# A graph-network kernel on one Trainium2 core: a later part's order of work, its loads and its last operations rearranged

## The chip, the cores and the metric

The kernel runs on one core of a Trainium2 chip. A core has five engines with queues of their own, which wait for each other by semaphores: PE (TensorE, matrix products into eight PSUM banks), DVE (VectorE), ACT (ScalarE), POOL (GpSimd, which here issues the gathers) and SP (SyncE, which issues most loads). The metric is the device time of one execution, in microseconds (us); lower is better.

## The reference, cut to what matters

x is 512 x 1024 in f32; 8192 edges (src, dst), sorted by dst, connect 512 nodes. `gnn` is the reference's first layer, cut to its formulas:

```python
h = relu(layernorm(x))
feat = concat([h[src], h[dst]], axis=1)
e_f = relu(feat @ W_kind + b_kind)          # kinds: first 256 edges hh, next 1280 oo, the rest ho
logit = e_f @ W_a + b_a
alpha = exp(logit - max[dst]); alpha = alpha / segment_sum(alpha, dst)[dst]
z_f = segment_sum(alpha * h[src], dst)
new = relu(concat([h, z_f]) @ W_node + b_node)   # W_hn for rows 0..127, W_on for the rest
x = x + new
h = relu(layernorm(x))
hW = h @ W.T + b
x = x + segment_sum(deg^-1/2[row] * deg^-1/2[col] * hW[col], row)   # with self loops
```

## The kernel before

**Edges.** The edges are handled in 64 tiles of 128: tiles 0 to 51 are kind ho, 52 to 61 oo, 62 and 63 hh. For the first two kinds the products of h with the halves of the weights are made once per node and stored as two tables in HBM (`tab_a`, `tab_b`). POOL gathers, for tile q, 128 rows of `tab_a` into a slot of `gath` (line 402) and then adds 128 rows of `tab_b` to it by a second, accumulating gather (`gather_add`, line 416), which first waits for the landing of the first. Odd tiles under 52 (`PLAIN`) gather both into two slots instead (lines 402 and 409). `gath` has `GB` = 9 slots, used in turn; a gather first waits until the tile that used its slot nine uses ago has been read by DVE (`slot_free`). The order on POOL is: first gather of q, then `gather_add` of q - 2 (`LAG`).

**One list of steps.** Behind the tables, PE, ACT and DVE walk through the same list of positions (c, k), with c a chunk of products and k = 0..7. Each engine executes in order, so what stands at a position holds up all that stands behind it on that engine. In chunks 12 and 13 PE also multiplies the node weights (line 845, fed by `round_w` on ACT, line 581, and `low_w` on DVE, line 1180). Chunks 14 and 15 hold no such products. At each position DVE does, in this order: `low_w`, `copy_kind`, `edge`, `split_logits`, `logit_onehots`.

- `edge(q)` (lines 1200 to 1205) waits for the gather of tile q, takes the relu, multiplies by W_a and sums to 128 logits. `EDGE_AT` (lines 506 to 511) says at which position. A plain tile takes one more operation.
- `split_logits` (line 1226 on, `SPLIT_AT`) cuts the logits into three bf16 parts `lgs`.
- `logit_onehots(q)` (lines 1242 to 1248) makes one-hot matrices of a tile's src and dst. For the tiles in `SCALED` (57, 59, 61) DVE also multiplies by the three parts (line 1245, three operations); for all others ACT does, in `logit_parts` (line 641, three operations), behind the one-hot's semaphore.
- `sums` on PE (line 795) adds a tile's logits, as products of one-hots, to a 512 x 512 matrix of logits for its kind. The order is `SUM_AT`: ..., 44 to 49, 62, 63, 50, 51, ..., 60, 61; it and the place of the one-hots are not touched.
- `copy_kind` on DVE (line 1270) brings a finished kind's four banks to SBUF with their row maxima; kind 1 (oo) is complete with the sum of tile 61.

**Behind the edges.** `head_rows` (line 1006) is a product of the first 128 rows of h in f32 with W_hn, 16 products by k (n = 0, 1). Its weights lie in the eight slots `raw`: those of n = 0 are loaded by SP once edge 55 is done, those of n = 1 and then the next weights (`load_behind_head`, line 323), each when the product that used the slot is done. Four of the 16 stand at position (15, 1), ahead of the sums of tiles 60 and 61. Then DVE and ACT make the softmax (lines 732, 736, 1400 to 1407), PE transposes the attention (line 1023) and multiplies it by h (line 1035, below called the z products), which it needs as two parts in rows, `hrow_h` and `hrow_l`. These lie over slots 1 to 8 of `gath` and are brought back from HBM by POOL: eight loads of 512 KB that wait for all edges and for the fourth head product (lines 455 to 459). Then follow the other node products (line 845), the residual and the second norm, the spreading of rows along edges (line 1066), the product with W (lines 845 and 1088), and the output (`outputs`, lines 1517 to 1532): from each bank two DVE operations with a wait between them, then a store by SP (line 345).

Of the kernel before, what the change touches and what calls it, by code (L numbers as in the profile page):

```python
# [5 lines left out]
P = 128  # L6
FB = 512
ALU = mybir.AluOpType
# [17 lines left out]
def gnn_kernel(nc, x, src, dst, W_hh, b_hh, W_oo, b_oo, W_ho, b_ho, W_a, b_a,  # L26
# [3 lines left out]
    NM = N // P  # L30
    KT = D // P
# [7 lines left out]
    with ExitStack() as ctx:  # L39
# [22 lines left out]
        hrow = sb("hrow", [P, NM, D], F32)  # L62
# [5 lines left out]
        GB = 9  # L68
# [282 lines left out]
        def _(pool):  # L351
# [103 lines left out]
            pool.wait_ge(s_edge, TG + GB)  # L455
            pool.wait_ge(s_hn, KT // 2)
            for m in range(NM):
                pool.dma_start(hrow_h[:, m, :], h_hi[m * P:(m + 1) * P, :]).then_inc(s_hld[m], 16)
                pool.dma_start(hrow_l[:, m, :], h_lo[m * P:(m + 1) * P, :]).then_inc(s_hld[m], 16)
# [46 lines left out]
        EDGE_AT |= {divmod(12 * KT + (3 * i) // 2, KT): (41 + i,) for i in range(10)}  # L506
        EDGE_AT |= {(14, k): (51 + k,) for k in range(KT)}
        EDGE_AT |= {(15, 0): (59,), (15, 1): (60, 61)}
# [25 lines left out]
        SCALED = (57, 59, 61)  # L534
# [241 lines left out]
        def _(pe):  # L776
# [234 lines left out]
            for c in (14, 15):  # L1011
                for k in range(KT):
                    sums(c, k)
                    if (c, k) == (15, 1):
                        head_rows(0, range(4))
            head_rows(0, range(4, KT))
# [75 lines left out]
        def _(dve):  # L1092
# [5 lines left out]
            def step(ins):  # L1098

                chain[0] += 1  # L1100
                ins.then_inc(s_v, 1)
                dve.wait_ge(s_v, chain[0])
# [413 lines left out]

            def outputs(n):
                c = slice(n * FB, (n + 1) * FB)
                if n == 0:
                    chunk_done(dve, q)  # L1520
                for m in range(NM):
                    if n:
                        dve.wait_ge(s_lastbank, m + 1)
                    step(nc.vector.scalar_tensor_tensor(out=topsum[:, m, c], in0=bias2[:, 0, c], scalar=wrow[:, m:m + 1],
                                                        in1=ps[:, n * NM + m, :], op0=ALU.mult, op1=ALU.add))
                    nc.vector.scalar_tensor_tensor(out=topsum[:, m, c], in0=topsum[:, m, c], scalar=dinv[:, m:m + 1],
                                                   in1=hrow[:, m, c], op0=ALU.mult, op1=ALU.add).then_inc(s_out, 1)

            outputs(0)
# [23 lines left out]
```

## Time and profile before

| | |
|---|---|
| median of 3 runs | 578.4 us (574.28 to 585.87) |
| profiled execution | 578.26 us |
| its span, first to last instruction | 576.5 us |
| its mean granted TensorE clock | 0.973 of full |
| VectorE busy | 418.3 us (73%) |
| GpSimd busy | 192.8 us (33%) |

The span is measured from the first to the last instruction; 1.8 us of the execution lie outside it. All places below are in us from the span's start. The profile's sections give busy time by engine, the granted clock by slice, the DMA queues (q0: POOL's; q1: SP's), the chain of work that ended last, and groups of instructions by line.

### The profile page before, as it was taken

To read this page: it belongs to the slowest core of one execution; us is meant where nothing else is said; L and a number is where in the kernel's file an instruction comes from. 1 tells how busy PE (TensorE), PEld (TensorE's weight loads), DVE (VectorE), ACT (ScalarE), POOL (GpSimd) and SP (SyncE) were. 2 spreads that over 40 slices of the span, in tenths; PEclk is the share of its full clock that TensorE was granted. 3 is DMA by queue.
4 is the path that set the end of the run, shared out by engine and by line. 5 is a ranking of instruction groups with operands and counts; after the bars stand their busy time and mean duration, and the time that the engine had idled before them with its cause. 6 is when DMAs were issued, how large, how long until landed. Compare 5 with 4: busy or idle time off the path is not lost.

```text
span 576.5 us, 7188 instructions
## 1 busy us (share of the span) xinstructions
PE 519.5 (90%) x2120; PEld 359.7 (62%) x2125; DVE 418.3 (73%) x883; ACT 273.1 (47%) x432; POOL 192.8 (33%) x177
## 2 busy tenths in 40 slices
PE   0799989999998799979999799996778999999997
PEld 0688857777764467644444368672226878878885
DVE  6766347874669789789888697589897389888262
ACT  1733431211223898945644662899366274144200
POOL 3290030007466475536655644584031000000000
PEclk9999999999999899998999977998899999999999
DMA  8899286449999999999999999999596575304021
GB/s 302 315 329 399 108 279 226 131 146 247 397 343 342 344 357 279 348 318 338 370 344 350 366 337 323 216 237 281 157 354 259 213 249 192 107 2 133 14 91 55
DMA packets 55838, 146.95 MB, mean 255 GB/s; under 512 B 6770, under 2 KB 6898, under 8 KB 55410
## 3 DMA queue, kind: packets, MB, share of 16 engines
q0 software_dynamic: 22352, 81.28, 45.7%
q1 hardware_dynamic: 27936, 54.54, 26.7%
q10 hardware_dynamic: 5506, 10.56, 5.0%
q8 instruction: 27, 0.44, 0.3%
q14 instruction: 17, 0.14, 0.1%
HBM read 127.47 MB, written 18.87 MB: 254 GB/s over the span
## 4 chain that ended last, share of the span: by engine, by line
PE 59%; DVE 16%; DMA 10%; ACT 7%; issue 5%; POOL 2%; ACTq 0%; DVEq 0%
PE ps L845 37%; PE ps L795 7%; DMA gath<-tab_a,tabl_i 6%; PE ps L1035 4%; PE ps L1088 4%; PE ps L1066 3%; DVE ring_l L1180 2%; ACT late_onehots L641 2%; ACT onehot L641 2%; DMA gath<-tab_b,tabl_i 2%; DVE gath L1205 1%; DVE logit_d L1400 1%; DMA raw<-in_L_gnn_W_on_dram 1%; DVE stats L1147 1%; POOL gath L409 1%
## 5 line engine op out<-in xcount | busy, mean ns | idle before, releaser
L845 PE MATMUL ps<-ring_h,actT_h 128*128 128x512 f32 x376 | 160.8, 428 | 7.5 <-DVE actT_l L1175 3.1
L845 PE MATMUL ps<-ring_l,actT_h 128*128 128x512 f32 x376 | 148.7, 395 | 0.0
L845 PE MATMUL ps<-ring_h,actT_l 128*128 128x512 f32 x376 | 148.7, 395 | 0.0
L641 ACT ACTIVATE onehot<-onehot,lgs 128x512 bf16<-128x512 bf16 x156 | 99.9, 711 | 45.9 <-DVE onehot L1248 38.7
L581 ACT CAST ring_h<-raw 128x512 fp32r<-128x512 f32 x128 | 76.2, 623 | 91.1 <-PE ps L845 63.6
L1180 DVE TENSOR_TENSOR ring_l<-raw,ring_h 128x512 fp32r<-128x512 f32 x128 | 85.4, 687 | 44.4 <-ACT ring_h L581 32.6
L402 POOL DMA_INDIRECT gath<-tab_a,tabl_i x62 | 66.9, 1079 | 100.1 <-DVE gath L1205 48.9
L416 POOL DMA_INDIRECT gath<-tab_b,tabl_i x36 | 64.9, 1801 | 87.5 <-DMA tab_b<-stage 43.6
L1205 DVE SCALAR_TENSOR_TENSOR gath<-gath,wa_b 128x1024 f32<-128x1024 f32 x62 | 75.8, 1225 | 21.0 <-DMA gath<-tab_b,tabl_i 20.1
L845 PEld LDWEIGHTS ps<-ring_h,actT_h 128*128 128x128 f32 x376 | 72.1, 192 | 30.3 <-DVE actT_l L1175 3.3
L845 PEld LDWEIGHTS ps<-ring_h,actT_l 128*128 128x128 f32 x376 | 71.8, 191 | 16.0
L845 PEld LDWEIGHTS ps<-ring_l,actT_h 128*128 128x128 f32 x376 | 72.1, 192 | 14.3
L795 PE MATMUL ps<-onehot 128*128 128x512 bf16 x230 | 64.5, 391 | 17.1 <-ACT onehot L641 13.7
L795 PEld LDWEIGHTS ps<-onehot 128*128 128x128 bf16 x233 | 19.1, 99 | 56.1 <-issue 45.1
L1200 DVE TENSOR_TENSOR gath<-gath 128x1024 f32<-128x1024 f32 x26 | 31.7, 1220 | 3.5 <-DMA gath<-tab_b,tabl_i 3.3
L409 POOL DMA_INDIRECT gath<-tab_b,tabl_i x26 | 30.4, 1170 | 7.9 <-issue 7.3
L943 PE MATMUL ps<-raw,featT_src 128*128 128x512 f32 x64 | 30.1, 610 | 0.0
L943 PE MATMUL ps<-raw,featT_dst 128*128 128x512 f32 x64 | 29.1, 592 | 0.0
L1128 DVE TENSOR_SCALAR onehot<-iota_f,node_f 128x512 bf16<-128x512 f16 x44 | 16.1, 367 | 14.4 <-PE ps L795 12.6
L599 ACT COPY stage<-ps 128x512 f32<-128x512 f32 x16 | 9.4, 585 | 24.7 <-PE ps L845 19.0
L943 PEld LDWEIGHTS ps<-raw,featT_src 128*128 128x128 f32 x64 | 12.7, 199 | 12.8 <-issue 11.2
L1006 PE MATMUL ps<-raw,hT 128*128 128x512 f32 x32 | 17.1, 669 | 3.5 <-DMA raw<-in_L_gnn_W_hn_dram 3.1
(206 smaller groups left out, 684.5 us busy)
## 6 DMA issues: line engine op xcount, KB each, us to landing
raw<-in_L_gnn_W_ho_dram SPq DMA_DIRECT2D x32, 256.0 KB
raw<-in_L_gnn_W_oo_dram SPq DMA_DIRECT2D x32, 256.0 KB
raw<-in_L_gnn_W_hh_dram SPq DMA_DIRECT2D x32, 256.0 KB
raw<-in_L_gnn_W_on_dram SPq DMA_DIRECT2D x32, 256.0 KB
raw<-in_L_gnn_W_hn_dram SPq DMA_DIRECT2D x32, 256.0 KB
tab_a<-stage ACTq DMA_DIRECT2D x16, 256.0 KB
tab_b<-stage ACTq DMA_DIRECT2D x16, 256.0 KB
raw<-in_L_gnn_W_dram SPq DMA_DIRECT2D x16, 256.0 KB
```

The source lines that it names most:

```text
L402: pool.indirect_dma_start(out=gath[:, c % GB, :], out_offset=None, in_=tab_a[0:kinds * N, :], in_offset=bass.IndirectOffsetOnAxis(ap=tabl_ ...
L409: pool.indirect_dma_start(out=gath[:, c % GB, :], out_offset=None, in_=tab_b[0:kinds * N, :], in_offset=bass.IndirectOffsetOnAxis(ap=tabl_ ...
L416: pool.indirect_dma_start(out=gath[:, c % GB, :], out_offset=None, in_=tab_b[0:kinds * N, :], in_offset=bass.IndirectOffsetOnAxis(ap=tabl_ ...
L581: nc.scalar.copy(ring_h[:, k, :], raw[:, k % RAW, :]).then_inc(s_high, 1)
L641: ins = nc.scalar.mul(place[:, 1 + i, :], place[:, 1, :], lgs[:, i, q:q + 1])
L795: mm = nc.tensor.matmul(ps[:, bass.ds(((lo + j) & 3) + first if first else (lo + j) & 3, 1), :].rearrange("p a n -> p (a n)"), rows[:, 1 + ...
L845: mm = nc.tensor.matmul(ps[:, first + m, :], w, v, start=(k == 0 and i == 0), stop=(k == KT - 1 and i == 2))
L943: mm = nc.tensor.matmul(ps[:, b, :], featT[half][:, k, t * P:(t + 1) * P], raw[:, k, :], start=(half == 0 and k == 0), stop=(half == 1 and ...
L1035: mm = nc.tensor.matmul(ps[:, f, :], w, v, start=(k == 0 and i == 0), stop=(k == NM - 1 and i == 2))
L1180: nc.vector.tensor_tensor(ring_l[:, k, :], raw[:, k % RAW, :], f32(ring_h[:, k, :]), ALU.subtract).then_inc(s_low, 1)
L1200: nc.vector.tensor_tensor(gath[:, c % GB, :], gath[:, c % GB, :], gath[:, d % GB, :], ALU.add).then_inc(s_sum, 1)
L1205: nc.vector.scalar_tensor_tensor(out=gath[:, c % GB, :], in0=gath[:, c % GB, :], scalar=0.0, in1=wa_b[:, :], op0=ALU.max, op1=ALU.mult, ac ...
```

## The change

1. **Edges.** `EDGE_AT` puts tiles 43 to 61 one to three positions further forward. Tiles 47 and 48 go from chunk 13 into chunk 12, 51 to 53 from chunk 14 to (13, 4), (13, 5) and (13, 7), 59 to 61 from chunk 15 to (14, 5), (14, 6) and (14, 7). One-hots, splits and sums stay.
2. **Scaling.** `SCALED` holds only tile 61; tiles 57 and 59 are scaled by ACT.
3. **Head.** Two instead of four head products stand ahead of the sums of tiles 60 and 61.
4. **Loads of h.** Each of the eight waits only for the edge that frees the slot it overwrites, in the order of the last nine uses: `hrow_h` blocks 2 and 3 behind edges 53 and 54, `hrow_l` 0 to 3 behind 56 to 59, `hrow_h` 0 and 1 behind 60 and 61. They stand behind the last `gather_add` on POOL, as before.
5. **Output.** The part that needs no PSUM (bias times a row factor plus the residual) is made by eight operations ahead of the outputs; from each bank one operation is left.

```diff
-            pool.wait_ge(s_edge, TG + GB)
-            pool.wait_ge(s_hn, KT // 2)
-            for m in range(NM):
-                pool.dma_start(hrow_h[:, m, :], h_hi[m * P:(m + 1) * P, :]).then_inc(s_hld[m], 16)
-                pool.dma_start(hrow_l[:, m, :], h_lo[m * P:(m + 1) * P, :]).then_inc(s_hld[m], 16)
+            for c in range(len(USES) - GB, len(USES)):
+                slot, q = c % GB, USES[c][0]
+                if slot == 0:
+                    continue
+                part, held = (hrow_l, h_lo) if slot <= NM else (hrow_h, h_hi)
+                m = (slot - 1) % NM
+                pool.wait_ge(s_edge, GB + q + 1)
+                pool.dma_start(part[:, m, :], held[m * P:(m + 1) * P, :]).then_inc(s_hld[m], 16)
...
-        EDGE_AT |= {divmod(12 * KT + (3 * i) // 2, KT): (41 + i,) for i in range(10)}
-        EDGE_AT |= {(14, k): (51 + k,) for k in range(KT)}
-        EDGE_AT |= {(15, 0): (59,), (15, 1): (60, 61)}
+        EDGE_AT |= {(12, k): (41 + k,) for k in range(KT)}
+        EDGE_AT |= {(13, k): (49 + i,) for i, k in enumerate((1, 2, 4, 5, 7))}
+        EDGE_AT |= {(14, k): (54 + k,) for k in range(KT)}
...
-        SCALED = (57, 59, 61)
+        SCALED = (61,)
...
                     if (c, k) == (15, 1):
-                        head_rows(0, range(4))
-            head_rows(0, range(4, KT))
+                        head_rows(0, range(2))
+            head_rows(0, range(2, KT))
...
+            step(nc.vector.tensor_tensor(wrow[:, :], wrow[:, :], dinv[:, :], ALU.mult))
+            def residuals(n):
+                c = slice(n * FB, (n + 1) * FB)
+                for m in range(NM):
+                    ins = nc.vector.scalar_tensor_tensor(out=topsum[:, m, c], in0=bias2[:, 0, c], scalar=wrow[:, m:m + 1],
+                                                         in1=hrow[:, m, c], op0=ALU.mult, op1=ALU.add)
+                step(ins)
             def outputs(n):
...
-                    step(nc.vector.scalar_tensor_tensor(out=topsum[:, m, c], in0=bias2[:, 0, c], scalar=wrow[:, m:m + 1],
-                                                        in1=ps[:, n * NM + m, :], op0=ALU.mult, op1=ALU.add))
-                    nc.vector.scalar_tensor_tensor(out=topsum[:, m, c], in0=topsum[:, m, c], scalar=dinv[:, m:m + 1],
-                                                   in1=hrow[:, m, c], op0=ALU.mult, op1=ALU.add).then_inc(s_out, 1)
+                    nc.vector.scalar_tensor_tensor(out=topsum[:, m, c], in0=ps[:, n * NM + m, :], scalar=dinv[:, m:m + 1],
+                                                   in1=topsum[:, m, c], op0=ALU.mult, op1=ALU.add).then_inc(s_out, 1)
+            residuals(0)
+            residuals(1)
             outputs(0)
             outputs(1)
```

## Rows read from the trace of the kernel before

**Rows 1.** The page's first part: busy us, share of the span, instructions of each engine.
```profile
PE 519.5 (90%) x2120; PEld 359.7 (62%) x2125; DVE 418.3 (73%) x883; ACT 273.1 (47%) x432; POOL 192.8 (33%) x177
```
**Rows 2.** The chain that ended last: start, us, what; from 410 on.
```profile
410.23 2.74 PE ps L795 x6
412.97 3.77 PE ps L1006 x8
416.74 1.31 PE ps L795 x6
418.08 0.69 DVE logit_d L1270
...
438.78 22.06 PE ps L1035 x96
```
**Rows 3.** Timeline of ACT: start, us, line, operation, operands, count, [idle before <-releaser].
```profile
375.81 7.46 ACT L641 ACTIVATE onehot<-onehot,lgs 128x512 bf16<-128x512 bf16 x12 [0.76 <-DVE onehot L1248]
...
397.47 7.45 ACT L641 ACTIVATE onehot<-onehot,lgs 128x512 bf16<-128x512 bf16 x12
...
412.54 1.95 ACT L641 ACTIVATE late_onehots<-late_onehots,lgs 128x512 bf16<-128x512 bf16 x3 [3.02 <-DVE late_onehots L1248]
```
**Rows 4.** Timeline of DVE, from 354 to 411, the rows that the steps use.
```profile
354.10 0.16 DVE L1376 COPY rs_in<-ps 128x4 f32<-128x4 f32 x1 [3.49 <-PE ps L973]
...
364.80 0.69 DVE L1180 TENSOR_TENSOR ring_l<-raw,ring_h 128x512 fp32r<-128x512 f32 x1 [4.66 <-ACT ring_h L581]
...
397.13 0.17 DVE L1226 TENSOR_SCALAR lgs<-lg 128x2 uint32<-128x2 uint32 x1
...
397.93 0.35 DVE L1242 TENSOR_SCALAR onehot<-iota_f,node_f 128x512 bf16<-128x512 f16 x1
...
398.99 1.22 DVE L1205 SCALAR_TENSOR_TENSOR gath<-gath,wa_b 128x1024 f32<-128x1024 f32 x1
...
402.13 1.05 DVE L1245 TENSOR_SCALAR late_onehots<-iota_f,node_f,lgs 128x512 bf16<-128x512 f16 x3
...
409.82 1.23 DVE L1205 SCALAR_TENSOR_TENSOR gath<-gath,wa_b 128x1024 f32<-128x1024 f32 x1
```
**Rows 5.** Timeline of POOL: an awaited slot, adds of tiles 58, 59, 61, first h load.
```profile
370.51 0.97 POOL L402 DMA_INDIRECT gath<-tab_a,tabl_i  x1 [4.59 <-DVE gath L1205]
...
386.61 1.54 POOL L416 DMA_INDIRECT gath<-tab_b,tabl_i  x1 [0.30 <-issue]
...
390.22 1.98 POOL L416 DMA_INDIRECT gath<-tab_b,tabl_i  x1 [0.68 <-DMA gath<-tab_a,tabl_i]
...
398.90 2.71 POOL L416 DMA_INDIRECT gath<-tab_b,tabl_i  x1 [3.40 <-DMA gath<-tab_a,tabl_i]
...
417.28 0.62 POOL L458 DMA_DIRECT2D hrow_h<-h_hi  x1 [15.67 <-PE ps L1006]
```
**Rows 6.** The instructions of tile gath, 330 to 415: from issue to landing.
```profile
DMA to landing us min/median/max: 9.3/10.4/11.5
```
**Rows 7.** Busy by stretch; its last three columns: granted clock, DMA share, GB/s.
```profile
358.00:376.00 18.00, 17.24 (x74) 12.69 (x73) 11.48 (x30) 12.42 (x21) 11.14 (x9) 0.97 0.90 202
```
**Rows 8.** SP's DMA queue, 380 to 400: packets, MB, share of 16 engines.
```profile
q1 hardware_dynamic: 323, 0.60, 8.6%
```
**Rows 9.** Busy by stretch again, here for PE and its granted clock (last but two).
```profile
352.00:359.00 7.00, 7.00 (x23) 5.94 (x23) 4.87 (x10) 1.09 (x2) 2.42 (x2) 0.51 1.04 324
...
406.50:410.20 3.70, 0.71 (x3) 0.10 (x1) 3.61 (x11) 1.95 (x3) 0.00 (x0) 0.99 0.61 162
410.30:413.60 3.30, 3.30 (x8) 1.36 (x9) 3.13 (x12) 1.06 (x2) 0.00 (x0) 0.51 0.00 0
```
**Rows 10.** Timeline of PE: the last two head products.
```profile
430.90 3.63 PE L1006 MATMUL ps<-raw,hT 128*128 128x512 f32 x4 [0.81 <-DMA raw<-in_L_gnn_W_hn_dram]
```
**Rows 11.** Timeline of DVE: the two operations of the last output bank.
```profile
572.43 0.75 DVE L1524 SCALAR_TENSOR_TENSOR topsum<-bias,wrow,ps 128x512 f32<-128x512 f32 x1 [3.90 <-PE ps L1088]
573.21 0.75 DVE L1526 SCALAR_TENSOR_TENSOR topsum<-topsum,dinv,hrow 128x512 f32<-128x512 f32 x1
```

## The prediction

> **What bounds it now.** I read the page's busy times first: PE 519.5 us, 90% of the span [rows 1]. The change touches no weight product, so it can only gain where the chain of waits leaves PE, and that chain was read next. From 376 to 405 it lies on ACT: the scaling of one-hots starts at 375.81 and the last unbroken group ends at 397.47 + 7.45 = 404.92, so the 15 tiles 44 to 49, 62, 63, 50 to 56 take 29.1 us with the bank copies between them, 7.45 / 4 = 1.86 a tile [rows 3]. After that DVE is late: ACT waits 3.02 for the one-hot of tile 60 and ends it at 412.54 + 1.95 = 414.49 [rows 3], for DVE is still reading edges at 409.82 + 1.23 [rows 4]. PE is later still: between sums 58/59 and 60/61 it makes four head products, 3.77 us, and 60/61 run from 416.74 [rows 2]. The copy of kind 1 follows at 418.08, and softmax and transposes take from there to the z products at 438.78: 20.7 us in which the chain lies on DVE and ACT [rows 2].
>
> Beside it run the gathers. The last add is issued at 398.90 [rows 5] and adds take 9.3 to 11.5 us to land [rows 6], so it lands at 408.2 to 410.4; the edge that needs it starts at 409.82 [rows 4]. It is just in time. The DMA engines are full in 352 to 359, share 1.04 [rows 9], and less so from 358 to 376, share 0.90 [rows 7], where POOL waits 4.59 us for an edge to free a slot [rows 5].
>
> **Edges, on DVE.** Edges 51 (two operations), 52 and 53 leave the full time behind 375. One operation takes 1.15 from start to start (410.96 - 409.82, the second operation being behind the first of [rows 4]), so this is 4 x 1.15 = 4.6 us. They, and 47 and 48 that enter chunk 12, are hidden in DVE's two waits of 3.49 at 354.10 and 4.66 at 364.80, which are for PE and for ACT's copies behind chunk 12 [rows 4]; without that cover they would cost 8 us. One is not hidden: edge 53 stands at (13, 7) ahead of the one-hot of tile 44, for which ACT waits at 375.81 with 0.76 idle [rows 3]. So ACT's run starts 1.15 later, at 376.95. Ended by ACT alone, tile 56 would be done at 376.95 + 29.1 = 406.05, and 57 to 60 follow.
>
> **Scaling.** DVE drops 2 x (3 - 1) operations of 1.05 / 3 = 0.35, some 1.4 us [rows 4]. ACT takes 2 x 1.86 = 3.7 us more. Its cover is the wait of 3.02 and a like one ahead of tile 58 [rows 3]. ACT alone would end tile 60 at 406.05 + 4 x 1.86 = 413.5, against 414.49.
>
> **Can the gathers follow?** This is the unknown. Edge 49, which freed the slot awaited for 4.59 us, now comes before DVE's wait at 364.80. Upper bound of what the last landings gain: about that wait, 4.6 us. Lower bound by the share: (1.04 - 0.90) / 1.04 x 18 = 2.4 us of unused DMA [rows 7, 9]; if W_hn's loads, which also start three positions earlier, eat it, none. I take 3.5, the middle of 2.4 and 4.6. The add of tile 58 is issued at 386.6 [rows 5]; with the median of 10.4 [rows 6] it lands at 397.0, and now at 393.5. From there DVE does edge 58 (1.15), a split of four small steps (397.93 - 397.13 = 0.8), two tiles' one-hots (398.99 - 397.93 = 1.06) [rows 4], four copies of kind 2 (at most 0.69 each [rows 2], 2.5 together), edge 59 (1.15), a split (0.8) and the one-hot of tile 54 (0.53): ready at 401.4. ACT then scales 54 to 60, 7 x 1.86 = 13.0: tile 60 at 414.4, tile 59 at 412.5. So the gathers still set the pace, 0.9 behind what ACT alone would allow.
>
> **Head on PE.** Sum 59 ends 0.7 (issue) + 0.65 after 412.5, at 413.9. Two head products, 3.77 / 2 = 1.9, end at 415.8; the two sums take 1.31 [rows 2] and end at 417.1. The copy of kind 1 starts there, against 418.08: **0.9 earlier**. Bounds: with ACT alone as limit 1.8 earlier; with no gain of the gathers, see the second rival, 1.9 later. The two head products moved back have cover there.
>
> **Loads of h.** They leave from about 396 on instead of 417.28 [rows 5], behind the last add on the same queue, and have landed by about 418; z needs them at 438. Their eight issues cost POOL nothing that anyone awaits. What changes is what they no longer disturb. Before, the last two head products waited for W_hn, and the head ended at 430.90 + 3.63 = 434.53 [rows 10], 4.2 ahead of z [rows 2]. Now 14 products at 0.94 from 417.1 end at 430.3. By the sum above z starts at 437.9, so PE has over 7 us with nothing but the attention's 16 small transposes. Before, there were 4.2 us between head and z, the transposes in it, and z ran at full speed, 22.06 / 96 = 0.23 a product [rows 2].
>
> **The clock.** After 3.70 us with 0.71 busy, at 0.99, the clock stood at 0.51, half speed (1.2 instead of 2.4 GHz), for the next 3.30 us, though PE was then fully busy; in another stretch for 7.00 us [rows 9]. So z now starts at half speed, where before it started at full. It costs half the slow time: 3.3 / 2 = **1.7 later**, upper bound 7.0 / 2 = 3.5 (there PE first made one-column products, so the 3.3 is nearer). z is a row of 96 products on the chain [rows 2]; all of it is passed on. The Trainium skill (TensorE: Matmul & The Clock Gate, section "HAM oscillation — how this bites in real kernels") sets the penalty at throttled time times (1 - 1.2/2.4) and warns of exactly such gaps; with its rule on the 7.00 us row the sum below would be 580.1 instead of 578.3. It is the rule that speaks against this change.
>
> **Output.** The last bank is followed by two operations, at 572.43 and 573.21 [rows 11]; one is left: **0.8 earlier** (573.21 - 572.43). Eight operations, which take two SBUF operands where those had one in PSUM, are added ahead at no more than 0.75 each, and eight go; up to the last bank DVE makes 9 + 7 = 16 operations where it made 14, at most 1.5 us more, and it waited 3.90 for that bank [rows 11]: hidden. Without that cover it would cost 1.5.
>
> **Sum.** The profiled execution took 578.26: 576.5 span and 1.8 around it. 578.26 - 0.9 + 1.7 - 0.8 = 578.3. The median of the runs shown is 578.4, so the two stand 0.1 apart.
>
> **Rivals.**
> *The clock holds.* If W_hn's second half still lands late, or transposes count enough, PE is not idle long enough, and the 1.7 fall away: 578.26 - 0.9 - 0.8 = 576.6; with ACT as the only limit 575.7. For it: transposes come in three lots. Against: 0.71 busy in 3.70 was too little to hold it [rows 9], and the h loads, 4 MB, are out of W_hn's way.
>
> *The gathers don't come earlier (slower).* Place: edge 59, now ahead of the one-hot of tile 54. Its add was issued at 390.22 [rows 5]; with the longest latency [rows 6] it landed at 401.7. If that stays, the one-hot of 54 is ready at 401.7 + 1.15 + 0.8 + 0.5 = 404.2, ACT ends 59 at 415.3 and 60 at 417.2, PE sum 59 at 416.7, head 418.6, sums 419.9, against 418.05: 1.9 later. Sum: 578.26 + 1.9 + 1.7 - 0.8 = 581.1. It decides against the change once the gathers gain less than about 2.6 of the 3.5 us (0.9 of gain used up). For it: share 1.04. Against: the unused 10% before 376. W_hn starts with edge 55 and moved only 0.60 MB of its 2.1 (eight loads of 256 KB) between 380 and 400, at 8.6% of the engines' time [rows 8]. The Trainium skill (DMA: Bandwidth & Descriptors, "Queues, rings and completion order") says each engine takes its queues in turn by packets; then W_hn, three positions earlier, pushes the last gathers back, and the outcome is this rival's 581.1. The 8.6% of [rows 8] is much less than an equal turn.
>
> *The middle does nothing.* ACT's later start and extra tiles use up the gain, and the clock holds: 578.26 - 0.8 = 577.5.
>
> **Chances.** Forecast (0 to 1.8 gained, cold z, 577.4 to 580): 0.45. Clock holds, with or without gain in the middle (575.7 to 577.5): 0.27. Gathers late (580 to 581.5, more if another slow stretch falls on the path): 0.20. Anything else, a scatter like that of the runs of before among it: 0.08. The range is 575.3 to 581.5: from the warm case with ACT as limit to the late gathers. A measurement of this kernel tells about 2%, 11.6 us, from no change; no case reaches it, and only scatter (the runs of before reach 585.87) gives 0.02 to faster and 0.03 to slower.
>
> **What would show it.** Right: ACT's scaling from about 377 without a break to about 414; the copy of kind 1 near 417; the h loads issued from 396 on; the head's end near 430 with no wait for W_hn; granted clock 0.5 for about 3 us from z's start; one DVE operation behind the last bank. Wrong: DVE idle on a gather in front of edges 54 to 61 with ACT idle behind it (late gathers); a granted clock of 1.00 through z; an edge in chunk 12 or 13 that makes PE wait for `ring_l`, which the sum puts at nothing.

## The result, and the profile after

| | before | changed |
|---|---|---|
| median | 577.89 us (4 runs, 574.28 to 585.87) | 583.63 us (4 runs, 580.29 to 586.01) |
| ratio | | 1.0092 [1.0052, 1.0133] |
| profiled execution, its span | 578.26, 576.5 | 583.28, 581.5 |
| mean granted clock in it | 0.973 | 0.959 |

The changed kernel is slower by about 0.9%, 5 us, and lies above the predicted range; by 2%, it counts as no change. A ratio, here and below, takes only the fast runs of a kernel (those within 1.5% of its own fastest), while the mean spans and fits below take every run, so that the two can differ by up to 0.5%. One correction to the account of the change: edges 51 and 52 move four positions forward, the others of 43 to 61 one to three. Lines of kernel.py from POOL's loads on are shifted by 3 (L1208 is the edge, L644 ACT's scaling, L1009 the head, L1038 the z products). All places are from the span's start.

First the chain of waits of the changed kernel (start, us, what), the counterpart of [rows 2]:

```profile
405.10 1.95 ACT onehot L644 x3
...
442.41 23.67 PE ps L1038 x96
```

z takes 23.67 where it took 22.06, and the chain now passes through ACT at 405.10, where ACT had been kept waiting. The timeline of ACT, counterpart of [rows 3]:

```profile
374.17 1.95 ACT L644 ACTIVATE onehot<-onehot,lgs 128x512 bf16<-128x512 bf16 x3
378.07 7.51 ACT L644 ACTIVATE onehot<-onehot,lgs 128x512 bf16<-128x512 bf16 x12 [1.95 <-DVE onehot L1251]
...
405.10 5.62 ACT L644 ACTIVATE onehot<-onehot,lgs 128x512 bf16<-128x512 bf16 x9 [1.92 <-DVE onehot L1251]
410.63 7.44 ACT L644 ACTIVATE late_onehots<-late_onehots,lgs 128x512 bf16<-128x512 bf16 x12
```

What ACT waits for is DVE's one-hot, and DVE stands in front of a gather (timeline of DVE, the edges of tiles 54 to 58, in brackets the wait ahead of each):

```profile
380.00 1.23 DVE L1208 SCALAR_TENSOR_TENSOR gath<-gath,wa_b 128x1024 f32<-128x1024 f32 x1 [1.44 <-DMA gath<-tab_b,tabl_i]
...
383.45 1.23 DVE L1208 SCALAR_TENSOR_TENSOR gath<-gath,wa_b 128x1024 f32<-128x1024 f32 x1 [0.95 <-DMA gath<-tab_b,tabl_i]
...
387.18 1.23 DVE L1208 SCALAR_TENSOR_TENSOR gath<-gath,wa_b 128x1024 f32<-128x1024 f32 x1 [1.12 <-DMA gath<-tab_b,tabl_i]
...
391.79 1.23 DVE L1208 SCALAR_TENSOR_TENSOR gath<-gath,wa_b 128x1024 f32<-128x1024 f32 x1 [0.70 <-DMA gath<-tab_b,tabl_i]
...
396.77 1.23 DVE L1208 SCALAR_TENSOR_TENSOR gath<-gath,wa_b 128x1024 f32<-128x1024 f32 x1 [2.69 <-DMA gath<-tab_b,tabl_i]
```

The view of DVE's waits from 330 to 440 sums them (us in total, times, longest):

```profile
DVE gath L1208 <- DMA gath<-tab_b,tabl_i: 11.3, 8, 3.2
```

In the profile of before there is no such wait in this stretch, and one of 1.1 us just ahead of it, at 328.6. Of the eight, five are those shown; the others stand ahead of tile 42 (0.9), which wasn't moved, ahead of tile 48 (3.2), and one of 0.3. On POOL the last add now leaves at 399.04 and the loads of h behind it from 400.01, as the counterpart of [rows 5] shows:

```profile
399.04 1.53 POOL L416 DMA_INDIRECT gath<-tab_b,tabl_i  x1 [3.52 <-DMA gath<-tab_a,tabl_i]
400.01 1.80 POOL L462 DMA_DIRECT2D hrow_h<-h_hi  x2
```

On PE, the sums up to 418.5 run at half clock (a sum of three products takes 1.46 where 0.82 is its time at full clock in the profile of out_only). The head behind them is at full clock and no longer waits for W_hn. z starts slowly: a product is recorded with 0.63 us, later with 0.40 (the records of neighbouring products overlap, so these are longer than the 0.23 from start to start):

```profile
416.94 1.46 PE L798 MATMUL ps<-late_onehots 128*128 128x512 bf16 x3 [0.38 <-issue]
...
426.99 7.83 PE L1009 MATMUL ps<-raw,hT 128*128 128x512 f32 x16 [0.30 <-PE ps L1009]
...
440.54 1.11 PE L1026 MATMUL ps<-ident,logit_d 128*128 128x128 f32 x4 [2.79 <-ACT logit_d L739]
...
445.14 0.63 PE L1038 MATMUL ps<-attT_h,hrow_h 128*128 128x512 f32 x1
...
446.15 0.40 PE L1038 MATMUL ps<-attT_h,hrow_h 128*128 128x512 f32 x1
```

The last bank is followed by one operation (timeline of DVE, counterpart of [rows 11]):

```profile
578.23 0.75 DVE L1537 SCALAR_TENSOR_TENSOR topsum<-ps,dinv,topsum 128x512 f32<-128x512 f32 x1 [4.69 <-PE ps L1091]
```

**Where the two profiles part.** Call a the place of DVE's first `low_w` of chunk 12; nothing ahead of it is changed, so what differs there is scatter. a is 320.9 before and 324.8 after: 3.9 of the 5.0 us between the spans lie ahead of all that was changed. Behind a: copy of kind 1 at a + 97.2 and a + 96.7; from it to z 20.7 and 20.8; z 22.0 and 23.7; from z's end to the end 115.7 and 115.4. Together that is the other 1.1 us, within rounding. So one pair of profiles can't settle this case. The comparisons below rest on twelve executions each (six or nine where said), and on these stretches in the one profile of each kernel.

### The profile page after: what moved, and what is told of

Same layout as the page of the kernel before. It is cut to its first block, busy times and chain, and to the rows that moved or that the text cites. A ratio compares the mean times of both kernels' runs of the same rounds, so it can differ in the third digit from the quotient of the medians.

```text
span 581.5 us, 7189 instructions
## 1 busy us (share of the span) xinstructions
PE 525.6 (90%) x2119; PEld 363.8 (63%) x2125; DVE 416.3 (72%) x880; ACT 277.2 (48%) x438; POOL 184.3 (32%) x177
## 4 chain that ended last, share of the span: by engine, by line
PE 53%; DMA 17%; DVE 14%; POOL 6%; issue 5%; ACT 3%; ACTq 1%; DVEq 0%
PE ps L848 33%; DMA gath<-tab_a,tabl_i 14%; PE ps L798 6%; PE ps L1038 4%; PE ps L1091 4%; PE ps L1069 3%; POOL gath L416 3%; DVE ring_l L1183 2%; DMA gath<-tab_b,tabl_i 2%; POOL gath L402 2%; DVE logit_d L1403 1%; POOL gath L409 1%; DMA raw<-in_L_gnn_W_on_dram 1%; PE ps L827 1%; ACT onehot L644 1%
## 5 line engine op out<-in xcount | busy, mean ns | idle before, releaser
L848 PE MATMUL ps<-ring_h,actT_l 128*128 128x512 f32 x376 | 150.3, 400 | 0.0
L644 ACT ACTIVATE onehot<-onehot,lgs 128x512 bf16<-128x512 bf16 x156 | 100.1, 710 | 55.7 <-DVE onehot L1251 52.2
L402 POOL DMA_INDIRECT gath<-tab_a,tabl_i x62 | 68.8, 1110 | 95.1 <-DMA tab_a<-stage 43.4
L1208 DVE SCALAR_TENSOR_TENSOR gath<-gath,wa_b 128x1024 f32<-128x1024 f32 x62 | 75.9, 1224 | 31.0 <-DMA gath<-tab_b,tabl_i 30.0
L416 POOL DMA_INDIRECT gath<-tab_b,tabl_i x36 | 62.0, 1723 | 94.9 <-DMA gath<-tab_a,tabl_i 45.9
L798 PE MATMUL ps<-onehot 128*128 128x512 bf16 x230 | 65.9, 398 | 17.9 <-ACT onehot L644 13.0
L409 POOL DMA_INDIRECT gath<-tab_b,tabl_i x26 | 31.7, 1220 | 7.9 <-issue 7.6
L644 ACT ACTIVATE late_onehots<-late_onehots,lgs 128x512 bf16<-128x512 bf16 x33 | 20.6, 712 | 0.1
```

The source lines that it names most:

```text
L402: pool.indirect_dma_start(out=gath[:, c % GB, :], out_offset=None, in_=tab_a[0:kinds * N, :], in_offset=bass.IndirectOffsetOnAxis(ap=tabl_ ...
L409: pool.indirect_dma_start(out=gath[:, c % GB, :], out_offset=None, in_=tab_b[0:kinds * N, :], in_offset=bass.IndirectOffsetOnAxis(ap=tabl_ ...
L416: pool.indirect_dma_start(out=gath[:, c % GB, :], out_offset=None, in_=tab_b[0:kinds * N, :], in_offset=bass.IndirectOffsetOnAxis(ap=tabl_ ...
L644: ins = nc.scalar.mul(place[:, 1 + i, :], place[:, 1, :], lgs[:, i, q:q + 1])
L798: mm = nc.tensor.matmul(ps[:, bass.ds(((lo + j) & 3) + first if first else (lo + j) & 3, 1), :].rearrange("p a n -> p (a n)"), rows[:, 1 + ...
L848: mm = nc.tensor.matmul(ps[:, first + m, :], w, v, start=(k == 0 and i == 0), stop=(k == KT - 1 and i == 2))
```

## The experiments

Each kernel is the kernel before with some of the five parts, or the changed kernel with some undone. "Half clock" is span x (1 - mean clock) x 2, the time in which TensorE stood at half clock, as a mean over the executions. The kernels ran in five groups, each with its own executions of before; "over its group" is the mean span above theirs, with its standard error.

| kernel | parts | ratio [95%] | mean span | over its group | half clock |
|---|---|---|---|---|---|
| before | | 1 | 576.7 (142) | | 33 |
| after_again | all | 1.0075 [1.0036, 1.0113] | 580.9 | +3.7 +- 0.9 | 44 |
| no_loads | all but loads | 1.0008 [0.9975, 1.0041] | 578.4 | +1.2 +- 0.8 | 38 |
| no_edges | all but edges | 1.0004 [0.9965, 1.0043] | 577.2 | 0.0 +- 1.0 | 39 |
| no_edges_loads | scaling, head, output | 1.0012 [0.9972, 1.0052] | 576.3 | -0.6 +- 1.0 | 36 |
| edges_only | edges | 1.0105 [1.0057, 1.0153] | 580.5 (6) | +3.6 +- 0.8 | 44 |
| edges_to50 | edges 43 to 50 | 1.0075 [1.0038, 1.0112] | 578.4 | +1.7 +- 0.9 | 35 |
| edges_to53 | edges 43 to 53 | 1.0045 [1.0011, 1.008] | 577.9 | +1.2 +- 1.1 | 34 |
| edges_from51 | edges 51 to 61 | 1.007 [1.0035, 1.0105] | 581.1 | +3.6 +- 0.8 | 39 |
| loads_only | loads | 1.0044 [1.0007, 1.0081] | 579.5 | +2.6 +- 1.3 | 42 |
| out_only | output | 0.995 [0.9909, 0.9991] | 575.0 | -2.3 +- 1.2 | 31 |
| out_again | output | 0.9985 [0.9944, 1.0025] | 577.1 | -0.4 +- 1.1 | 36 |
| out_head | output, head | 0.9983 [0.9947, 1.0019] | 575.2 | -1.4 +- 1.1 | 32 |
| out_scaled | output, scaling | 1.0051 [1.0013, 1.0088] | 576.9 | +0.3 +- 1.0 | 37 |

A least-squares fit of every execution of these kernels, the partial edge moves left out (256 spans, one effect per part), gives edges +3.1 +- 0.7 us, loads +2.2 +- 0.6, scaling +0.6 +- 0.8, head -1.1 +- 0.8, output -0.7 +- 0.6 (standard errors). The sum is 4.1; the changed kernel measured 580.9 - 576.7 = 4.2. With only the executions that the ratios use the effects are +3.4, +1.6, +1.5, -1.0 and -0.5, each +- 0.5 to 0.6. If the half-clock time of each execution is put into the fit of all 256 as well, the time grows by 0.33 us for each us of it, and what is left of the parts is edges +1.2 +- 0.4, loads +0.2 +- 0.4, scaling -0.1 +- 0.5, head -0.3 +- 0.5, output -0.8 +- 0.4: nearly all that the loads cost, and 1.9 of the edges' 3.1 us, goes with half-clock time.

**The whole again, and one part undone.** The diffs are the parts of the change shown above, left as they were before.

after_again: 

> The changed kernel again, with more rounds. Its first profile was 5.0 us longer than the one of before, but 3.9 of that had already arisen at place 320, ahead of anything the change touches; from there the middle gained 0.5, the z products lost 1.6 at half clock, the stretch behind them 0.6, and the end gained 0.8. Theory A (scatter of the clock ahead of 320): the loss shrinks with more runs, to a ratio of 1.001 to 1.004. Theory B (the loss is made behind 320 in most runs, by late gathers and by slow clock, more than in the one profile): the ratio stays near 1.009, and this profile shows more than 2 us lost from place 320 on.

no_loads: 

> The changed kernel with the eight loads of h as before (behind all edges and the fourth head product). Theory 1 (cold z: early loads free W_hn, the head ends early, PE idles and z starts at half speed): 1.6 to 3 us faster than the changed kernel, head products again wait for W_hn, z takes 22.1 us instead of 23.7. Theory 2 (late gathers): the same time as the changed kernel within 1 us, and z's clock is of no account.

no_edges: 

> The changed kernel with the edges at the old positions; loads of h, scaling, head and output changed. Theory 2 (edges too far forward, DVE waits for gathers with ACT idle behind it): 1 to 3 us faster than the changed kernel. Theory 1 (cold z): within 1 us of it, and z still starts at half speed.

The loss is real, and with one of two parts undone the ratio is 1.0008 or 1.0004. So no single part carries it.

**Parts alone.**

out_only: 

> The kernel before with only the output changed: eight operations ahead, one behind each bank. All theories: 0.8 us faster than before (573.21 - 572.43 in the trace), a ratio of 0.9986, within the scatter. If something in the layout of the program itself costs time, it shows here as a loss.

no_edges_loads: 

> The kernel before with scaling, head and output changed, edges and loads of h as before. Theory 1 + 2 (edges and early loads each cost some 2 to 4 us, the other three parts gain): a ratio of 0.993 to 0.997, z in 22.1 us at full clock, one-hot of tile 44 scaled 5.2 us behind that of tile 42 and tile 60 36.1 us behind that of 44. Rival (the two parts only cost something together with the others): a ratio of 1.000.

edges_only: 

> The kernel before with only the edges moved. Theory 2 (edge 53 stands ahead of the one-hot of tile 44, 1.15 us, and the gathers of 54 to 58 land late, 0 to 2 us): tile 44 is scaled 6.4 us behind tile 42 instead of 5.2, DVE waits for gathers in front of edges 48 and 54 to 58, ratio 1.002 to 1.006. Rival (the moved edges alone gain, as tiles 58 and 60 no longer wait for DVE, and only together with the scaling on ACT do they lose): ratio below 1.000.

loads_only: 

> The kernel before with only the loads of h changed: each waits for the edge that frees its slot. Theory 1: the head ends 3 us or more earlier, z starts at half clock and takes 23.7 to 24.8 us, ratio 1.003 to 1.006. Rival (the cold start needs the moved edges or the split head too): z 22.1 us and a ratio of 1.000.

Edges alone cost most, 1.0105. Loads alone cost 1.0044, and z takes 24.5 in its profile. Scaling, head and output together measured 1.0012, within 0.5% of none.

**Is it the cold start of z?** Ten products of zeros ahead of each of the last three lots of transposes:

```diff
             for m in range(NM):
+                if m:
+                    for _ in range(10):
+                        nc.tensor.matmul(ps[:, 0, :], zeros_r[:, 0:P], zeros_r[:, :], start=True, stop=True, skip_group_check=True)
                 pe.wait_ge(s_att, m + 1)
```

after_warm: 

> The changed kernel with ten products of zeros into an idle bank ahead of each of the transposes of row blocks 1, 2 and 3 of the attention (2.3 us of PE each at full clock), so that PE has work while the softmax runs. Theory 1 (z loses its time by the clock): z takes 22.1 us instead of 23.7 to 24.8, and the ratio falls from 1.0075 to 1.003 to 1.005. Rival (z is slow by what the early loads do to memory, or the loads cost elsewhere): z stays at 23.7 or more, and the time stays or grows.

Measured 1.01 [1.0049, 1.0152] (6 runs, mean span 580.2): nothing won that shows. z is at full clock in the profile, 22.05, but starts 23.4 behind the copy of kind 1 instead of 20.8: thirty products take 3 x 2.32 = 7 us, more than PE had idle there. So a fill that fits the idle time, on the loads alone (7 ahead of the third lot, 10 ahead of the fourth):

```diff
+                for _ in range((0, 0, 7, 10)[m]):
+                    nc.tensor.matmul(ps[:, 0, :], zeros_r[:, 0:P], zeros_r[:, :], start=True, stop=True, skip_group_check=True)
```

loads_fill: 

> The kernel before with the early loads of h and with products of zeros in PE's waits between the transposes, 7 (1.6 us) ahead of the third lot and 10 (2.3 us) ahead of the fourth. Theory (what the early loads cost is the cold start of the z products and no more): z in 22.1 us instead of 24.5, start of z 20.7 to 20.9 behind the copy of kind 1, ratio 0.999 to 1.001, where loads_only had 1.0044. Rival (the loads cost elsewhere, among the gathers): z in 22.1, ratio 1.003 or more.

Timeline of PE of loads_fill: the last lot, then z:

```profile
438.58 2.32 PE L1025 MATMUL ps<-zeros_r 128*128 128x512 bf16 x9
441.54 0.66 PE L1028 MATMUL ps<-ident,logit_d 128*128 128x128 f32 x4 [0.63 <-ACT logit_d L739]
443.26 0.50 PE L1040 MATMUL ps<-attT_h,hrow_h 128*128 128x512 f32 x1 [1.07 <-DVE attT_l L1175]
...
443.83 0.39 PE L1040 MATMUL ps<-attT_h,hrow_l 128*128 128x512 f32 x1
```

z takes 22.09 and starts 20.69 behind the copy. Over all profiles: with the early loads z took 23.7, 24.8, 23.7 and 24.5, with 3.4 to 5.8 us of it at half clock; with them and a fill 22.05 to 22.09 in three of three; with the old loads 22.04 to 22.09 in nine of thirteen, and 23.5 to 24.9 in four. These four are edges_only, edges_from51, edges_fill and out_fill; none of the seven with edges 51 to 61 at their old places and no fills is among them, so the moved edges may cost at this place too, which no run tests.

That the early loads make z start cold, and that a fitting fill takes this away, is shown. That the whole kernel gets the time back is not: the ratio is 0.9992 [0.9946, 1.0038], on six executions, and overlaps the 1.0044 [1.0007, 1.0081] of loads_only; over all twelve the mean span is 577.5 against 579.5, but measured from their own groups the two stand at +2.0 +- 1.1 and +2.6 +- 1.3. What speaks for the clock as the whole cost of the loads is the fit: 2.2 +- 0.6 us, of which 0.2 +- 0.4 are left at equal half-clock time.

**What makes the edges cost?** First the half-clock time. Over the 142 executions of the kernel before, a span grows by 0.33 us for each us at half clock (correlation 0.83), and the changed kernel has 11 us more of it: 3.6 us of the 4.2, if that is the cause. In the profile of edges_only a stretch of 10.2 us at half clock falls on the last sums and the first head products. From tile 44's start on ACT to the copy of kind 1 the seven profiles with edges up to 53 or further moved and no fills there have 13.7 to 17.1 us at half clock, the nine with the old order 3.4 to 17.1, on average 8.3. Products of zeros ahead of the sums, added to the bank that is being summed:

```diff
+            FILL = {q: 3 for q in (51, 53, 54, 55, 56)} | {58: 8, 60: 8}
             def add_logits(q, place):
+                for _ in range(FILL.get(q, 0)):
+                    nc.tensor.matmul(ps[:, KIND_BANK[kind_of(q)], :], zeros_r[:, 0:P], zeros_r[:, :], start=False, stop=False, skip_group_check=True)
```

out_fill: 

> The kernel before with the output change and with products of zeros, which change nothing in the result, ahead of the sums of tiles 51, 53 to 56 (three each) and 58 and 60 (eight each), where PE waits for ACT or DVE. Theory (over the runs of one kernel the time grows by 0.33 us for each us in which TensorE is at half clock, and the half-clock time in the sums and the head comes from PE's waits there): the granted clock stays at 1.00 from tile 52's sum to the head's end, the mean clock rises by 0.005 or more over out_only's 0.973, ratio 0.990 to 0.994. Rival (DVE and ACT set the pace of the sums, so PE's clock there changes nothing): 0.995 as out_only. Rival (the products of zeros stand in the way of the sums): 0.998 or more.

edges_fill: 

> The kernel before with the moved edges and with the products of zeros of out_fill ahead of the same sums. Theory (the moved edges cost by PE's waits for tiles 54 to 60 and the half clock that follows in the sums and the head, 10 us of it in the profile of edges_only): the clock holds there, ratio 0.998 to 1.004 instead of 1.0105, mean clock 0.968 or more instead of 0.962. Rival (late gathers and edge 53 hold up ACT by themselves): ratio 1.006 or more at a mean clock as high.

after_fills: 

> The changed kernel with both sets of products of zeros. Theory (3.5 of the 4 us that the change costs are half-clock time): ratio 0.997 to 1.001 and a mean clock of 0.970 or more, against 1.0075 and 0.962. Rival (the order of the edges costs by itself): ratio 1.004 or more at that clock.

Measured: out_fill 1.0067 [1.0029, 1.0106] at a mean clock of 0.971, edges_fill 1.0153 [1.0115, 1.0191] at 0.969 (6 runs), after_fills 1.0089 [1.0059, 1.0118] at 0.974 (9 runs). The fills are in the way: the mean span of out_fill, 578.6, is 2.5 +- 1.2 us above that of out_only and out_again, and its clock isn't higher. Most of this has a place. The fills of tile 58 stand in a wait, but those of tile 60 stand directly behind the head products, where PE had none. The chain of out_fill (start, us, what: head, an issue, the fills, of which seven are recorded, the sums of 60 and 61):

```profile
418.70 3.43 PE ps L1011 x8
422.13 0.05 issue
422.19 1.67 PE ps L898 x7
423.86 1.31 PE ps L795 x6
```

In after_fills the half-clock time falls from 44 to 30 us and the span only from 580.9 to 579.4, with 1.7 us of fills at the same place. So the fills are no clean test of what half clock is worth in the sums. One comparison is left, within one group: edges_fill is 4.6 us above out_fill, 3.9 +- 1.1 without the output part, at half-clock times of 36 and 34 us. Here the edges cost as much as without fills, though the clock is alike. That, and the 1.2 +- 0.4 left in the fit, speak against the clock as the only way in which they cost.

Then which of the edges. In edges_to50 51 to 61 stay where they were, in edges_to53 54 to 61, and edges_from51 leaves 41 to 50:

```diff
 # edges_to50
+        EDGE_AT |= {(12, k): (41 + k,) for k in range(KT)}
+        EDGE_AT |= {(13, k): (49 + i,) for i, k in enumerate((1, 2))}
 # edges_from51
+        EDGE_AT |= {(13, 5): (50, 51), (13, 6): (52,), (13, 7): (53,)}
+        EDGE_AT |= {(14, k): (54 + k,) for k in range(KT)}
```

edges_to50: 

> The kernel before with only edges 43 to 50 moved forward as in the change; 51 to 61 stay. Theory (the cost of the edges lies in the last tiles, where the gathers are awaited, and in edge 53 ahead of the one-hot of tile 44): none of the two is in this kernel, so ratio 0.996 to 1.002, no gather waits behind edge 49 of over 1 us, ACT's run from tile 44 starts 5.2 us behind tile 42's. Rival (the earlier edges in chunk 12 cost, by holding back low_w and so PE): ratio 1.005 or more.

edges_to53: 

> The kernel before with edges 43 to 53 moved forward as in the change; 54 to 61 stay. Theory: edge 53 now costs ACT 1.15 us at the start of its run (6.3 instead of 5.2 us behind tile 42), the gathers of 54 to 61 are not awaited: ratio 1.000 to 1.004, some 1.2 us above edges_to50. Rival (all of the cost lies in the waits for the gathers of 54 to 58): the same as edges_to50. Rival (all of it is edge 53 and what stands ahead of it): as edges_only, 1.0105.

edges_from51: 

> The kernel before with the complement of edges_to50: edges 51 to 53 at the end of chunk 13 and 54 to 61 in chunk 14 as in the change, 41 to 49 where they were and 50 at (13, 5). Theory (the cost of the moved edges is that edge 53 holds up the one-hot of tile 44 by 1.15 us and that edges 54 to 58 wait for their gathers ahead of one-hots that ACT needs, 2.3 us): ratio 1.004 to 1.008, ACT starts tile 44 some 1.1 us later behind tile 43 than in the kernel before, and tile 58 some 34.5 instead of 32 us behind tile 44. Rival (the moves of 43 to 50 in chunk 12 carry the cost): ratio 0.998 to 1.002.

edges_from51 measured 1.007, in the range of the theory of the late gathers and edge 53. The timeline of ACT of out_again, which has the old order, first; tile 44 starts at 373.55 and nothing breaks the row:

```profile
370.84 1.95 ACT L641 ACTIVATE onehot<-onehot,lgs 128x512 bf16<-128x512 bf16 x3
373.55 7.46 ACT L641 ACTIVATE onehot<-onehot,lgs 128x512 bf16<-128x512 bf16 x12 [0.76 <-issue]
...
386.88 9.30 ACT L641 ACTIVATE late_onehots<-late_onehots,lgs 128x512 bf16<-128x512 bf16 x15
396.08 7.44 ACT L641 ACTIVATE onehot<-onehot,lgs 128x512 bf16<-128x512 bf16 x12
```

The same timeline of edges_from51, tiles 43 and 44 and from tile 52 on:

```profile
372.44 1.95 ACT L641 ACTIVATE onehot<-onehot,lgs 128x512 bf16<-128x512 bf16 x3 [2.48 <-DVE onehot L1248]
377.35 7.46 ACT L641 ACTIVATE onehot<-onehot,lgs 128x512 bf16<-128x512 bf16 x12 [2.96 <-DVE onehot L1248]
...
398.82 1.95 ACT L641 ACTIVATE late_onehots<-late_onehots,lgs 128x512 bf16<-128x512 bf16 x3 [1.54 <-DVE late_onehots L1248]
400.68 1.93 ACT L641 ACTIVATE onehot<-onehot,lgs 128x512 bf16<-128x512 bf16 x3
404.52 5.62 ACT L641 ACTIVATE onehot<-onehot,lgs 128x512 bf16<-128x512 bf16 x9 [1.92 <-DVE onehot L1248]
```

Its waits are 2.48, 2.96, 1.54 and 1.92. In this kernel edges 51 to 53 stand closer together ahead of the one-hots of 43 and 44 than in the change, so its first two waits are longer. DVE's waits for gathers in out_again, 330 to 440 (us in total, times, longest):

```profile
DVE gath L1205 <- DMA gath<-tab_b,tabl_i: 0.2, 1, 0.2
```

And in edges_from51:

```profile
DVE gath L1205 <- DMA gath<-tab_b,tabl_i: 8.3, 5, 3.7
```

The same steps in all profiles but those of out_fill and after_fills (us; "44" and so on is the start of ACT's scaling of a tile):

| profile of | a to copy of kind 1 | of it at half clock | 43 to 44 | a to 44 | 44 to 58 | 44 to end of 60 | end of 60 to copy |
|---|---|---|---|---|---|---|---|
| before | 97.2 | 20.5 | 2.71 | 54.9 | 31.8 | 38.7 | 3.6 |
| out_only | 90.4 | 6.8 | 2.62 | 48.8 | 32.4 | 39.3 | 2.3 |
| out_again | 91.4 | 6.8 | 2.71 | 49.7 | 32.4 | 39.3 | 2.3 |
| out_head | 95.2 | 13.7 | 2.71 | 52.1 | 33.9 | 40.8 | 2.3 |
| out_scaled | 93.6 | 10.2 | 2.71 | 49.9 | 31.9 | 38.1 | 5.7 |
| loads_only | 93.7 | 17.1 | 2.71 | 51.6 | 31.6 | 38.6 | 3.6 |
| loads_fill | 96.2 | 23.9 | 2.71 | 50.8 | 34.2 | 41.1 | 4.3 |
| no_edges | 92.9 | 17.1 | 2.72 | 52.6 | 31.8 | 38.0 | 2.3 |
| no_edges_loads | 95.2 | 20.5 | 2.71 | 53.1 | 33.6 | 39.8 | 2.3 |
| edges_to50 | 94.1 | 10.2 | 2.85 | 52.7 | 32.2 | 39.1 | 2.3 |
| edges_to53 | 99.8 | 27.3 | 3.90 | 55.6 | 33.0 | 40.0 | 4.2 |
| edges_from51 | 100.6 | 20.5 | 4.91 | 54.7 | 34.5 | 39.0 | 6.9 |
| edges_only | 99.1 | 23.9 | 3.78 | 53.2 | 34.4 | 38.9 | 7.0 |
| no_loads | 97.6 | 23.9 | 3.78 | 53.3 | 33.9 | 39.5 | 4.8 |
| after | 96.7 | 23.9 | 3.90 | 53.2 | 34.4 | 40.0 | 3.5 |
| after_again | 98.1 | 30.7 | 3.78 | 57.2 | 32.5 | 38.1 | 2.7 |
| after_warm | 98.0 | 20.5 | 3.91 | 52.6 | 35.2 | 40.8 | 4.6 |
| edges_fill | 98.4 | 13.7 | 3.90 | 53.0 | 34.8 | 39.3 | 6.2 |

With the old order the stretch from a is 90.4 to 97.2 long in all nine profiles, on average 94.0; with edges up to 53 or further moved it is never under 96.7, and with all of them moved and no fills ahead of the sums (five profiles) 97.9 on average. Where are the 3.9 us?

- Ahead of tile 44: 2.4 (a to 44, 53.9 against 51.5). Of these, 1.1 to 1.2 are edge 53 ahead of the one-hot of 44, in every profile that has it at (13, 7). The rest has no cause shown.
- From 44 to the end of tile 60: 0.2 (39.5 against 39.3), but who scales 57 and 59 must be kept apart. With DVE scaling them the three profiles with edges 54 to 61 moved (edges_from51, edges_only, edges_fill) have 38.9 to 39.3, the six with the old order 38.6 to 41.1: ACT's new waits, 1.9 us ahead of tile 54 among them, take the place of its old ones of 2.3 to 2.6 and 3.0 us ahead of tiles 58 and 60. With ACT scaling them, as in the change, the old order has no such waits, and the run takes 39.6 on average against 38.6; after_again, where DVE waits 4.1 us for gathers instead of 11.3 to 11.8, has 38.1. So the waits for gathers add some 1 us here, and take away what the move was to gain.
- From the end of tile 60 to the copy: 1.3 (4.5 against 3.2). This is PE's part, sums and head products, and here much of the half-clock time lies.

Two things stay open. edges_to50 measured 1.0075 (span +1.7 +- 0.9), and its profile has none of these losses. It shows DVE waiting 2.6 us for the gather of tile 42 and PE behind it 4.2 us for DVE (line 1217); but tile 42 wasn't moved, and with the old order these waits are 0.2 to 2.4 and 0 to 3.9. And edges_to53 is not above it, where the theory wanted 1.2 us more; the two intervals overlap by too much to tell.

**Scaling and head**, each on the output part:

out_scaled: 

> The kernel before with the output change and with tiles 57 and 59 scaled by ACT instead of DVE. Theory (with the edges where they were, ACT is the last to be ready, so two tiles more on it, 3.7 us, use up its 3.0 us of waiting, and more): ratio 0.998 to 1.002, some 2 us above out_only's 0.995. Rival (the scaling is hidden): 0.995.

out_head: 

> The kernel before with the output change and two instead of four head products ahead of the sums of 60 and 61. By the chain of the kernel before the sums follow the head directly, so this gives 1.9 us: ratio 0.992, 4.5 us under before, where out_only has 0.995. Rival (PE has made the head products by the time that ACT has tile 60 ready in most executions, so the order is free): 0.995 as out_only.

Measured 1.0051 [1.0013, 1.0088] and 0.9983 [0.9947, 1.0019]. By its ratio, scaling on ACT without the moved edges loses against out_only and out_again (0.995, 0.9985), as its theory said; by mean spans it stands 0.9 +- 1.1 us above them, and over all kernels the fit can't tell its 0.6 +- 0.8 from nothing. Of the head's 1.9 us nothing is certain either (-1.1 +- 0.8).

out_again: 

> The kernel of out_only once more, the only one under 1 so far. If the output change is worth what its one operation less is worth, 0.8 us, the ratio is 0.9986; if it is worth what out_only showed, 0.995. Either way it would be the best version of the two kernels and their parts.

0.9985 [0.9944, 1.0025]; with out_only the two mean spans, 575.0 and 577.1, lie on both sides of before's 576.7. By the fit the output part is worth 0.7 +- 0.6 us. It is the best of the versions run, by less than these runs can prove.

## Why the prediction was wrong, step by step

- **Output, predicted 0.8 earlier.** Right: one operation behind the last bank, the stretch from the spreading to the end is 70.2 in out_only, out_again and out_head, 70.4 in the changed kernel, and 71.0 before; the fit gives 0.7 +- 0.6.
- **Cold z, predicted 1.7 later.** Right in mechanism and size: 1.6 in the profile, 1.6 to 2.7 in four, the loads' effect 2.2 +- 0.6; a fitting fill makes z warm again. The head's end, predicted at 430.3, that is a + 109.4, came at a + 110.0. The Trainium skill (TensorE: Matmul & The Clock Gate, section "HAM oscillation — how this bites in real kernels") warns of such gaps; its warning held here, and so did its rule of half the throttled time: 3.4 us at half clock in z cost 1.6, 5.8 us cost 2.7. The 3.5 us that the prediction got from it took the 7.00 us row as the throttled time, which was longer than what fell on z.
- **Edge 53 ahead of tile 44's one-hot, predicted 1.15 on ACT.** Right: (tile 43 to 44) 3.90 - 2.71 = 1.19.
- **Gathers, predicted to land 3.5 earlier.** Against the profile of before the steps came out: ready for tile 54 at 401.4, that is a + 80.5 (measured a + 80.3); end of tile 60 at 414.4, a + 93.5 (a + 93.2); copy of kind 1 at 417.1, a + 96.2 (a + 96.7). The last add, too, left at a + 74.2 where before's left at a + 78.0. But this agreement is luck: no gather came earlier by the change. Over the nine profiles with the old order the last add left at a + 72.0 to 78.0, over the five with all edges moved at a + 73.5 to 74.4, and both means are 74.0. With the old order DVE waits 0.2 to 2.4 us for gathers behind a, all of it for tile 42; with the new one it reaches the edges sooner and stands there for 11.3 to 11.8 us in four of five profiles. This is what the rival of the late gathers described, at its place, ahead of the one-hot of tile 54. Its price is smaller than the waits: some 1 us of ACT's run.
- **PE behind DVE in chunks 12 and 13, put at nothing.** No profile shows PE waiting there for `ring_l`. This part of the sum isn't refuted.
- **Head and scaling.** The sum had them as hidden. Neither can be told from nothing over all executions (-1.1 +- 0.8 and +0.6 +- 0.8), though scaling is +1.5 +- 0.6 on those that the ratios use.

**The step that failed** is the term of 0.9 earlier for the middle, in two ways. First its baseline. The sum was made against before's own execution, and that its 578.26 agreed with the median of 578.4 seemed to make it typical. It was so in total only: the part ahead of a was short (320.9; 320.3 to 326.6 in the others), and the middle was the longest of all with the old order (97.2; the others 90.4 to 96.2), with 20.5 us at half clock in it. [rows 9] show two such stretches, and the prediction read them as fixed. They are so in part: of the 20 profiles 14 have a half-clock stretch near a + 31, where the first of the two stands, but ten of the 14 have 3.4 us where before had 6.8. Second, the gain of the gathers, which isn't there. In profiles with little half-clock time the old order reached the copy at a + 90 to 91, and the new one never before a + 96.7. Measured, the middle's term is +3.1 +- 0.7 instead of -0.9, and with the loads' 2.2, the output's -0.7, scaling's +0.6 and head's -1.1 the sum is 4.1 above before's mean. In the profiles edge 53 accounts for 1.2 us, which the prediction had and thought paid for, and the late gathers for some 1; in the fit 1.9 of the 3.1 us go with half-clock time. How far these are the same microseconds, and why the moved edges bring more half-clock time, stays open.

**The range.** The late-gather rival had 0.20 and the price of 581.1, worked out from the same long middle: it put the loss there at 1.9. Against the old order's mean of 94.0, the new 97.9 is 3.9 more. The range left out scatter as well: the times of the kernel before run from 571.8 to 586.2 in one group.

## What to carry to other kernels

One profiled execution that agrees with the median can hide a short part and a long one; when the clock changes within the run, take a stretch's length from several executions before a step is costed against it. Moving a consumer further forward in an in-order queue pays only where its data are already there: look at whether its data are waiting for it. Here the edges started just as their gathers landed, and moved forward they stood for 11.3 us in the queue, with one-hots behind them that ACT needed, which used up what the move was to gain. When a phase ends early, look at what TensorE does until its next product, and what clock that product gets.

## What the runs showed of the hardware

- The same program's span varies from one execution to the next (standard deviation 3.1 us over 142), and two thirds of its variance go with the time TensorE spends at half clock: 0.33 us per us, where a product bound by PE would lose 0.5. At equal half-clock time 1.8 us of scatter are left.
- The half-clock stretches in the profiles mostly lasted 3.4, 6.8 or 10.2 us. They come back at a few places of the program (near a + 11, a + 31, a + 60, a + 80 to 90 and a + 110 to 120), but not in each execution and not with the same length. They fell also amid full work: PE was busy for all 7.00 us of the first stretch of [rows 9].
- Products of zeros cost what they take where PE has no wait: 1.7 us for the eight ahead of tile 60's sum, of the 2.5 +- 1.2 that all 31 cost in out_fill. Thirty where PE had less idle time delayed z by 2.6 us (after_warm), 17 that fitted didn't delay it (20.69 behind the copy, loads_fill). The mean clock didn't rise in out_fill (0.971); it did in after_warm (0.962 to 0.972) and after_fills (0.974), where the mean spans are 0.8 and 1.6 us shorter than in after_again.
